# A two-layer recurrence on one core: a new order of work in the step, and input products in tiles of 64 stationary columns

## The chip, the core and the metric

The kernel runs on one core of a Trainium2 chip. The metric is device time of one launch in microseconds, the median of several runs. In this text PE is TensorE (matmuls), PEld its weight loads, DVE is VectorE, ACT is ScalarE, POOL is GpSimd and SP is SyncE, which here only issues DMAs. A "record" is one line of the trace for a matmul or a weight load: each fp32 matmul instruction of the program leaves two matmul records and two weight-load records.

## The reference, cut to what matters

Four layers follow each other, each added to its input (batch 32, 256 time steps, 256 features). The first two are recurrences over time and are what the change touches:

```python
# layer 0, for each t
z = sigmoid(x_t @ W_z + h @ U_z + vz)
r = sigmoid(x_t @ W_r + h @ U_r + vr)
hh = tanh(x_t @ W + (r * h) @ U + vh)
h = (1.0 - z) * h + z * hh            # x1_t = x_t + h
# layer 1, for each t
gate = sigmoid(g @ Wh.T + x1_t @ Wz.T + b)
g = tanh(g * (1 - alpha) + gate * x1_t)   # x2_t = x1_t + g
```

Layers 2 and 3 (a scan with forget and input gates, and an adapter with low-rank factors) have no loop over time on PE. They run after the recurrence and the change leaves them as they are.

## The kernel before

All arithmetic is fp32. The 256 features lie on 128 partitions in 2 halves (index m for an output half, k for an input half). A step t of layer 0 and a step t - 3 of layer 1 are done together (LAG is 3). The program unrolls 16 steps (BODY) in a hardware loop on DVE, ACT and POOL, and 4 steps (LOOP) in a hardware loop on PE.

**Tiles on PE.** For the recurrent products (`quarter`, L770) the stationary operand is a block of 128 rows by 32 columns of a weight, placed in one of four column positions, and the moving operand is the state, 128 by 32. One `quarter` is 4 matmuls, one for each position (8 records), and covers one (k, m). A step has 8 quarters of layer 0's gates r and z, 4 of the candidate and 4 of layer 1's gate: 16 quarters, 128 records. The products of the inputs (`ahead`, L714) don't depend on the state. They are made for two steps at once, so their moving operand is 128 by 64, with the same 32-column stationary blocks; per step they are 64 records (48 of `ahead_first` with wx, 16 of `ahead_second` with wz). They accumulate in PSUM on top of seeds (constants and biases) which ACT writes with copies (L333, L336, L339).

**Order on PE in a step** (`turn`, L824): the gates (`first_gates`, L778: half 0 of the state first, then half 1; then the rest, z last), one short piece of input products, layer 1's gate (`second_gate`, L797), the candidate (`first_cand`, L809) with 8 records of input products in the hole between its first and second quarter, and then the other input products, which stand between the candidate and the gates of the next step.

**The other engines.** ACT makes r from PSUM in two halves (L360), z (L362) and 1 - z by a second sigmoid with scale -1 (L363), layer 1's gate (L375), the candidate by tanh in two halves (L369), seeds, and layer 1's state by tanh (L380). DVE makes r h in two halves (L570), (1 - z) h (L572), gate times x1 (L602), the new state by two scans (L582), layer 1's sum by one scan (L608) and x1 (L596). POOL adds x2 (L267). Who waits for whom is written out by hand with semaphores; each engine runs its list in order. SP loads x for the input products in blocks of two steps, each released by the z products of an earlier step (L204), and x for the residual in blocks of eight steps (L196).

Of the kernel before, what the change touches and what calls it, by code (L numbers as in the profile page):

```python
# [13 lines left out]
HALVES, SLABS, BLK = 2, 4, 32  # L14
SLAB = D // SLABS
# [13 lines left out]
def build_program(nc, io):  # L29
# [3 lines left out]
    with ctx:  # L33
# [6 lines left out]
        def sem(name):  # L40
# [21 lines left out]
        keep_f = sb("keep_f", [P, HALVES, B])  # L62
# [29 lines left out]
        idle = sb("idle", [P, 2 * LAG])  # L92
# [25 lines left out]

        banks = [pb(f"bank{n}", [P, 512]) for n in range(8)]
# [11 lines left out]
        scanned, bits_set, seeds_ready, bias_done, hid_copied = (  # L131
            sem("scanned"), sem("bits_set"), sem("seeds_ready"), sem("bias_done"), sem("hid_copied"))
        seeded = sem("seeded")
# [19 lines left out]
        pad_done = sem("pad_done")  # L153
# [31 lines left out]
        def _(sp):  # L185
# [16 lines left out]
            def next_turn(n, others=()):  # L202
# [8 lines left out]
                next_steps(n, 1)  # L211


            next_turn(0, [(dst[:], io[name], tail_in) for dst, name in TAIL_LOADS])
# [42 lines left out]
        def _(pool):  # L257
            pool.memset(rin_g[:], 0.0).then_inc(pad_done, 1)

            pool.sem_inc(x2_done, 1)  # L260
            pool.sem_inc(y_done, FREE)

            def turn(n):
                for u in range(BODY):
                    s = n * BODY + u
                    pool.wait_ge(gate_pre, s + LAG + 2)
# [3 lines left out]
            with nc.Fori(0, TURNS, engines=bass.OrderedEngineSet([pool.engine]), hint_back_edge=True) as n:  # L270
                turn(n)
            pool.wait_ge(w2_used, 4)
# [43 lines left out]
        def _(act):  # L316
# [12 lines left out]
            def seed_reset(par, cands=None):  # L329
                for m in range(HALVES):  # L330
                    if cands is not None:
                        act.wait_ge(cand_done, cands + m)
                    act.activation(flat(pre_rh[par][m]), flat(seed_rh[:, m]), ACT.Copy).then_inc(seeded, 1)  # L333
# [4 lines left out]
            def seed_gate(par):  # L338
                act.activation(flat(pre_g[par]), flat(seed_g[:]), ACT.Copy).then_inc(seeded, 1)  # L339
# [3 lines left out]
            seed_reset(0)  # L343
            seed_keep(0)
            seed_reset(1)
            seed_gate(1)
# [9 lines left out]
            def gates_first(n, u):  # L356
                t, par, v = n * BODY + u, (u // STEPS) % 2, u % STEPS
                for m in range(HALVES):
                    act.wait_ge(r_pre, 2 * t + m + 1)
                    act.activation(r_f[:, m], pre_rh[par][m][:, 0, v, :], ACT.Sigmoid).then_inc(r_done, 1)  # L360
                act.wait_ge(z_pre, t + 1)
# [712 lines left out]
```

## Time and profile before

| | |
|---|---|
| median of 3 runs | 992.34 us (991.52 to 993.38) |
| profiled execution, its own time | 988.54 us |
| its span in the profile | 986.7 us |
| PEld busy | 763.6 us (77%) |
| ACT busy | 647.4 us (66%) |
| POOL busy | 203.3 us (21%) |

The profile's page gives for each engine the busy time, its share of the span and the number of instructions. The recurrence fills the first 612 us of the span; layers 2 and 3 fill the rest.

### The profile page before, as it was taken

What the parts mean: (1) busy time and instruction counts of PE and PEld (TensorE: products, weight loads), DVE (VectorE), ACT (ScalarE), POOL (GpSimd) and SP (SyncE); (2) the same over time, 40 slices, a digit from 0 to 9 for tenths busy, and PEclk for the clock granted to TensorE, in tenths of its full rate; (3) what the DMA queues carried; (4) which work ended last, traced back from release to release, by engine and by line L of the source; (5) the groups of instructions that cost most, each with busy time, mean ns of one, the idle gap of its engine ahead of it and who ended that gap; (6) DMA issues with size and microseconds to landing.
All of it is one profiled execution on the core that took longest, in us unless ns stands there. A gap on an engine that the chain in (4) does not pass through costs nothing.

```text
span 986.7 us, 112657 instructions
## 1 busy us (share of the span) xinstructions
PE 939.5 (95%) x50966; PEld 763.6 (77%) x50966; DVE 803.9 (81%) x2468; ACT 647.4 (66%) x2862; POOL 203.3 (21%) x390
## 2 busy tenths in 40 slices
PE   5699999999999999999999999959999999999986
PEld 5699999999999999999999998325555555555554
DVE  2378778878788778777878887799999999999993
ACT  2477777777777777777777776336455556555552
POOL 0011111111111111111111111223333223323330
PEclk7699999999999999999999999979999999999999
DMA  6113312310010100100101001100010000001001
GB/s 219 41 57 111 111 47 98 110 35 27 24 37 24 37 24 27 35 27 24 37 24 37 24 27 33 28 1 25 24 42 29 24 24 24 24 24 48 24 24 43
DMA packets 38295, 42.02 MB, mean 43 GB/s; under 512 B 5120, under 2 KB 31232, under 8 KB 37120
## 3 DMA queue, kind: packets, MB, share of 16 engines
q1 hardware_dynamic: 36832, 40.55, 13.3%
q10 hardware_dynamic: 1440, 1.18, 0.4%
q8 instruction: 12, 0.20, 0.1%
q14 instruction: 11, 0.09, 0.0%
HBM read 32.80 MB, written 8.91 MB: 42 GB/s over the span
## 4 chain that ended last, share of the span: by engine, by line
PE 55%; DVE 31%; issue 8%; ACT 4%; DMA 1%; ACTq 1%; DVEq 1%; POOL 0%; POOLq 0%
PE bank L772 30%; PE bank L718 22%; DVE arena L645 10%; DVE wx L657 4%; DVE cx L661 4%; ACT cand_kept L369 2%; DVE cx L670 2%; DVE cx L674 2%; DVE wx L643 2%; DVE cx L666 2%; DVE none_h L582 2%; DMA bias<-in_bias 1%; PE bank L890 1%; PE bank L907 1%; PE bank L861 1%
## 5 line engine op out<-in xcount | busy, mean ns | idle before, releaser
L718 PE MATMUL bank<-x_ahead,wx 128*32 128x64 f32 x12376 | 345.6, 224 | 6.4 <-ACT bank L336 3.2
L718 PEld LDWEIGHTS bank<-x_ahead,wx 128*32 128x32 f32 x12376 | 240.1, 111 | 3.3 <-issue 3.3
L772 PE MATMUL bank<-none_h,urz 128*32 128x32 f32 x16384 | 203.2, 199 | 8.6 <-issue 5.0
L772 PEld LDWEIGHTS bank<-none_h,urz 128*32 128x32 f32 x16384 | 180.8, 110 | 27.7 <-DVE none_h L582 13.2
L267 POOL TENSOR_TENSOR x<-x_f,h_gx 128x64 f32 x256 | 87.4, 341 | 529.9 <-PE bank L772 528.8
L890 PE MATMUL bank<-x,wl 128*128 (+1 forms) x384 | 180.9, 610 | 0.9 <-DVE rank_rows L624 0.9
L772 PE MATMUL bank<-rh_f,uh 128*32 128x32 f32 x8192 | 151.6, 199 | 5.0 <-DVE rh_f L570 2.2
L890 PEld LDWEIGHTS bank<-x,wl 128*128 128x128 f32 x384 | 68.7, 190 | 88.1 <-issue 88.1
L772 PEld LDWEIGHTS bank<-rh_f,uh 128*32 128x32 f32 x8192 | 122.7, 112 | 7.1 <-DVE rh_f L570 5.3
L582 DVE TENSOR_TENSOR_SCAN none_h<-zero_z,cand_kept 128x64 f32<-128x64 f32 x512 | 121.4, 278 | 5.4 <-ACT cand_kept L369 4.0
L380 ACT ACTIVATE h_gx<-h_pre 128x64 f32<-128x64 f32 x256 | 68.8, 269 | 80.8 <-DVE h_pre L608 80.8
L772 PE MATMUL bank<-h_gx,wh 128*32 128x32 f32 x8288 | 121.0, 198 | 0.7 <-ACT h_gx L380 0.7
L423 ACT ACTIVATE arena<-bank,bl 128x512 f32<-128x512 f32 x96 | 65.9, 687 | 77.5 <-PE bank L890 77.3
L570 DVE TENSOR_TENSOR rh_f<-r_f,none_h 128x32 f32<-128x32 f32 x512 | 82.4, 192 | 40.3 <-ACT r_f L360 19.3
L369 ACT ACTIVATE cand_kept<-bank 128x32 f32<-128x32 f32 x512 | 99.1, 202 | 21.0 <-PE bank L772 9.0
L645 DVE RECIPROCAL arena<-wx 128x512 f32<-128x512 f32 x32 | 107.3, 3353 | 1.1
L572 DVE TENSOR_TENSOR cand_kept<-keep_f,none_h 128x64 f32<-128x64 f32 x256 | 60.3, 235 | 58.6 <-ACT keep_f L363 56.9
L608 DVE TENSOR_TENSOR_SCAN h_pre<-zero_leak,h_gx 128x128 f32<-128x128 f32 x256 | 102.0, 399 | 0.1
L772 PEld LDWEIGHTS bank<-h_gx,wh 128*32 128x32 f32 x8288 | 95.6, 112 | 4.1 <-ACT h_gx L380 1.8
L718 PE MATMUL bank<-x_f,wz 128*32 128x64 f32 x4128 | 88.4, 223 | 0.0
L360 ACT ACTIVATE r_f<-bank 128x32 f32<-128x32 f32 x512 | 79.1, 190 | 9.4 <-PE bank L772 9.4
L279 POOL TENSOR_TENSOR arena<-arena 128x512 f32<-128x512 f32 x32 | 40.6, 1269 | 210.1 <-ACT arena L423 195.5
(87 smaller groups left out, 1290.0 us busy)
## 6 DMA issues: line engine op xcount, KB each, us to landing
x_in<-in_x SPq DMA_DIRECT2D x34, 256.0 KB, 2.7
x_ahead<-in_x SPq DMA_DIRECT2D x130, 64.0 KB, 1.9
arena<-in_w SPq DMA_DIRECT2D x8, 1024.0 KB, 5.7
out<-y SPq DMA_DIRECT2D x32, 256.0 KB, 2.5
rank_rows<-in_bias_rows SPq DMA_DIRECT2D x1, 1024.0 KB, 5.0
arena<-scratch SPq DMA_DIRECT2D x64, 16.0 KB
cx<-in_cx SPq DMA_DIRECT2D x1, 768.0 KB, 4.5
wx<-in_wx SPq DMA_DIRECT2D x1, 768.0 KB, 6.6
```

What stands on the lines that cost most here:

```text
L267: pool.tensor_tensor(x2[:, :, :, s], x1_f[:, u % LOOP], h1_gx[:, u % 2, :, :, 0], ALU.add).then_inc(x2_done, 1)
L360: act.activation(r_f[:, m], pre_rh[par][m][:, 0, v, :], ACT.Sigmoid).then_inc(r_done, 1)
L369: act.activation(cand_kept[:, u % 2, m, :, 0], pre_rh[par][m][:, 1, v, :], ACT.Tanh).then_inc(cand_done, 1)
L380: act.activation(h1_gx[:, at, :, :, 0], h1_pre[:, at, :, :, 1], ACT.Tanh).then_inc(h1_done, 1)
L423: act.activation(dst[:, unit], banks[(at + 2 * par) % 4][:], fun, bias=bl2[:, mat, unit:unit + 1]).then_inc(done, 1)
L570: dve.tensor_tensor(rh_f[:, m], r_f[:, m], none_h[:, now, m, :, 1], ALU.mult).then_inc(rh_done, 1)
L582: dve.tensor_tensor_scan(pairs(none_h, m), pairs(zero_z, m), pairs(cand_kept, m), 0.0, ALU.mult, ALU.add).then_inc(h_done, 1)
L608: dve.tensor_tensor_scan(flat(h1_pre[:, at]), flat(zero_leak[:]), flat(h1_gx[:, 1 - at]), 0.0, ALU.mult, ALU.add).then_inc(pre1_done, 1)
L645: dve.reciprocal(rec[:, k], s_t).then_inc(rec_done, 1)
L718: mm = pe.matmul(out[32 * j:32 * j + 32], weights(k, j, m), moving(k), start=False, stop=False, tile_position=(0, 32 * j), skip_group_chec ...
L772: mm = pe.matmul(out[32 * j:32 * j + 32], weights(k, j, m), moving(k), start=False, stop=k == 1, tile_position=(0, 32 * j), skip_group_che ...
L890: mm = pe.matmul(banks[(at + 2 * par) % 4][:], wl2[:, k, mat, unit], x2[:, k, bass.ds(p * GB, GB), :].rearrange("p q t -> p (q t)"), start ...
```

## The change

* **Tiles.** The input products go in stationary blocks of 64 columns instead of 32 (`WIDE`), two column positions instead of four, with half as many matmuls. Only the first block of the prologue keeps 32 columns. The weights wx and wz are copied once by POOL into the layout for that (`widen`, 8 copies, into the space of cx and of y), and PE waits for the 8 copies before its first step. The recurrent products keep blocks of 32 columns.
* **Order on PE.** Gates, then a block of input products (8 matmuls, 16 records), then the candidate, then layer 1's gate, then a second block of input products (16 records). No input product stands inside the gates or the candidate any more. In the gates both r quarters of state half 0 come first and the second r quarter of half 1 follows the first at once.
* **(z - 1) h.** The sigmoid of -z on ACT (L363) goes. DVE makes (z - 1) h from z by one instruction; the candidate's tanh has scale -1, and the state's scan subtracts.
* **Layer 1** moves half a step later on DVE and ACT: gate times x1 and its scan are done at the head of the next step on DVE, the tanh after r on ACT, and the matmuls for its gate behind the candidate's. x1 is made behind r h of the next step, without a wait of its own for layer 1's scan.
* **Seeds and waits.** The seeds of r and candidate go behind layer 1's gate on ACT, and PE waits for them (`reset_seeded`). POOL's x2 waits for z in place of layer 1's products. SP issues the second half's residual load of the turn before behind the fourth x block. r_done and cand_done are counted down by PE.

```diff
+WIDE = 2 * BLK
...
+        wx_wide = cx[:].rearrange("p k j g e -> p (k j g e)").rearrange("p (g k m n) -> p g k m n", g=3, k=HALVES, m=HALVES)
+        wz_wide = y[:, 0].rearrange("p h t -> p (h t)").rearrange("p (k m n) -> p k m n", k=HALVES, m=HALVES)
...
+                    if c == 3 and not first:
+                        next_steps(n - 1, 1)
...
+            def widen(dst, src):
+                slabs = lambda w: w.rearrange("p j (m c) -> p m j c", m=HALVES)
+                pool.tensor_copy(dst.rearrange("p m (j c) -> p m j c", j=SLABS), slabs(src)).then_inc(widened, 1)
+
+            pool.wait_ge(wx_in, 16)
+            pool.wait_ge(const_pre, 1)
+            for gate in (0, 2):
+                for k in range(HALVES):
+                    widen(wx_wide[:, gate, k], wx[:, k, :, gate])
+            pool.wait_ge(weights_in, 16 * len(WEIGHT_LOADS + SECOND_LOADS))
+            for k in range(HALVES):
+                widen(wz_wide[:, k], wz1[:, k])
+            for k in range(HALVES):
+                widen(wx_wide[:, 1, k], wx[:, k, :, 1])
...
+                    if last and u >= BODY - LAG - 1:
+                        pool.wait_ge(gate_pre, s + LAG + 2)
+                    else:
+                        pool.wait_ge(z_done, s + LAG + 2)
...
                 act.activation(zero_z[:, u % 2, :, :, 1], pre_z[par][:, :, v, :], ACT.Sigmoid).then_inc(z_done, 1)
-                act.activation(keep_f[:], pre_z[par][:, :, v, :], ACT.Sigmoid, scale=-1.0).then_inc(z_done, 1)
...
-                                   ACT.Tanh).then_inc(cand_done, 1)
+                                   ACT.Tanh, scale=-1.0).then_inc(cand_done, 1)
...
+                    t = n * BODY + u
+                    reset_gate(n, u)
+                    if not first or u > LAG:
+                        second_state(n, u)
+                    elif u:
+                        act.activation(idle[:, u:u + 1], var_eps[:], ACT.Copy).then_inc(h1_done, 1)
+                    update_gate(n, u)
+                    if u % STEPS == 0 and (u or not first):
+                        if first and u <= LAG + 1:
+                            act.wait_ge(gate_pre, u - 1)
+                        else:
+                            act.wait_ge(gate_done, t - LAG - 1)
+                        seed_gate(((u - STEPS) // STEPS) % 2)
+                    candidate(n, u)
+                    if not first or u >= LAG:
                         second_gate(n, u)
-                    candidate(n, u)
-                    t = n * BODY + u
                     if u % STEPS:
-                        seed_reset((u // STEPS) % 2, 2 * t + 2)
+                        if first and u < LAG:
+                            act.activation(idle[:, 0:1], var_eps[:], ACT.Copy).then_inc(idle_done, 1)
+                            act.wait_ge(idle_done, 1)
+                        else:
+                            act.wait_ge(gate_done, t - LAG + 1)
+                        seed_reset((u // STEPS) % 2, reset_seeded)
                     else:
-                        if second or u:
-                            act.wait_ge(z_done, 2 * t)
+                        if u or not first:
+                            act.wait_ge(z_done, t)
                         seed_keep(1 - (u // STEPS) % 2)
-                        if second:
-                            act.wait_ge(gate_done, t - LAG + 1)
-                        else:
-                            act.wait_ge(gate_pre, u + 1)
-                        seed_gate(((u - LAG) // STEPS) % 2)
-                    if second:
-                        second_state(n, u)
-                    else:
-                        act.activation(idle[:, u:u + 1], var_eps[:], ACT.Copy).then_inc(h1_done, 1)
...
+            def kept_state(n, u):
                 t, now = n * BODY + u, (u + 1) % 2
-                for m in range(HALVES):
-                    dve.wait_ge(r_done, 2 * t + m + 1)
-                    dve.tensor_tensor(rh_f[:, m], r_f[:, m], none_h[:, now, m, :, 1], ALU.mult).then_inc(rh_done, 1)
-                dve.wait_ge(z_done, 2 * t + 2)
-                dve.tensor_tensor(cand_kept[:, u % 2, :, :, 1], keep_f[:], none_h[:, now, :, :, 1],
-                                  ALU.mult).then_inc(kept_done, 2)
+                dve.wait_ge(z_done, t + 1)
+                dve.scalar_tensor_tensor(cand_kept[:, u % 2, :, :, 1], zero_z[:, u % 2, :, :, 1], 1.0,
+                                         none_h[:, now, :, :, 1], ALU.subtract, ALU.mult).then_inc(kept_done, 1)
...
-                                           0.0, ALU.mult, ALU.add).then_inc(h_done, 1)
-
-            def first_output(n, u, first):
+                                           0.0, ALU.mult, ALU.subtract).then_inc(h_done, 1)
...
-                    reset_state(n, u)
-                    if second:
+                    if not first or u > LAG:
                         second_gated(n, u)
+                        second_sum(n, u)
+                    reset_state(u)
+                    if u:
+                        first_output(n, u - 1, first)
+                    elif not first:
+                        first_output(n - 1, BODY - 1)
+                    kept_state(n, u)
                     next_state(n, u)
-                    if second:
-                        second_sum(n, u)
-                    first_output(n, u, first)
...
+            def ahead(out, weights, moving, width):
+
+                for k in range(HALVES):
+                    for at in range(0, P, width):
+                        mm = pe.matmul(out[at:at + width], weights(k, at), moving(k), start=False, stop=False,
+                                       tile_position=(0, at), skip_group_check=True)
                 return mm
...
+                narrow = lambda k, at: wx[:, k, at // BLK, gate, m * BLK:(m + 1) * BLK]
+                wide = lambda k, at: wx_wide[:, gate, k, m, at:at + WIDE]
+                return ahead(out.rearrange("p v b -> p (v b)"), narrow if first else wide,
+                             lambda k: x_ahead[:, par, :, k, :], BLK if first else WIDE)
...
+                    ahead(pre_g[par][:, m].rearrange("p v b -> p (v b)"), lambda k, at: wz_wide[:, k, m, at:at + WIDE],
+                          lambda k: x1_f[:, at:at + STEPS, k, :], WIDE)
...
+            pe.wait_ge(widened, 8)
...
                 pe.wait_ge(h_done, 1)
                 reset(0, 0)
-                keep(0, 0)
-                keep(0, 1)
+                pe.wait_ge(cand_done, 2)
+                reset(0, 1)
+                update(0, 0)
                 pe.wait_ge(h_done, 2)
-                reset(1, 0, taken=h_done).then_inc(r_pre, 1)
-                reset(0, 1)
+                reset(1, 0, taken=(h_done, cand_done)).then_inc(r_pre, 1)
                 reset(1, 1).then_inc(r_pre, 1)
-                keep(1, 0)
-                mm = keep(1, 1)
-                if late_keep:
-                    mm = late_keep()
-                mm.then_inc(z_pre, 1)
+                update(0, 1)
+                update(1, 0)
+                update(1, 1).then_inc(z_pre, 1)
...
                 pe.wait_ge(rh_done, 1)
                 cand(0, 0)
-                hole()
                 pe.wait_ge(rh_done, 2)
-                cand(1, 0).then_inc(cand_pre, 1)
-                cand(0, 1).then_inc(rh_done, -2)
+                cand(1, 0, taken=(rh_done, r_done)).then_inc(cand_pre, 1)
+                cand(0, 1)
                 cand(1, 1).then_inc(cand_pre, 1)
...
             def turn():
-                first_gates(0, late_keep=lambda: ahead_first(0, 1, 1, (1,)))
-                second_gate(0)
-                first_cand(0, hole=lambda: loaded(1, 0, 0, (0,)))
-                ahead_second(LOOP - STEPS, 1)
-                ahead_first(1, 0, 0, (1,))
-                ahead_first(1, 0, 1)
-
-                first_gates(1)
-                ahead_first(1, 2, 0, (0,))
-                second_gate(1)
-                first_cand(1, hole=lambda: ahead_first(1, 2, 0, (1,)))
-                ahead_first(1, 2, 1)
-                ahead_first(1, 1, 0)
-                ahead_first(1, 1, 1, (0,))
-
-                first_gates(2, late_keep=lambda: ahead_first(1, 1, 1, (1,)))
-                second_gate(2)
-                first_cand(2, hole=lambda: loaded(0, 0, 0, (0,)))
-                ahead_second(0, 0)
-                ahead_first(0, 0, 0, (1,))
-                ahead_first(0, 0, 1)
-
-                first_gates(3)
-                ahead_first(0, 2, 0, (0,))
-                second_gate(3)
-                first_cand(3, hole=lambda: ahead_first(0, 2, 0, (1,)))
-                ahead_first(0, 2, 1)
-                ahead_first(0, 1, 0)
-                ahead_first(0, 1, 1, (0,))
+                for u in range(LOOP):
+                    later = 1 - u // STEPS
+                    first_gates(u)
+                    if u % STEPS == 0:
+                        pe.wait_ge(ahead_loaded[later], 16)
+                        pe.wait_ge(reset_seeded, 2)
+                        ahead_first(later, 0, 0)
+                        ahead_first(later, 0, 1).then_inc(reset_seeded, -2)
+                    else:
+                        ahead_second((u - LAG) % LOOP, later)
+                    first_cand(u)
+                    second_gate(u)
+                    if u % STEPS == 0:
+                        ahead_first(later, 2, 0)
+                        ahead_first(later, 2, 1)
+                    else:
+                        ahead_first(later, 1, 0)
+                        ahead_first(later, 1, 1).then_inc(ahead_loaded[later], -16)
```

## Rows read from the trace of the kernel before

**Rows 1.** The page: busy time of two engines, share, instructions.
```profile
PE 939.5 (95%) x50966; PEld 763.6 (77%) x50966; DVE 803.9 (81%) x2468; ACT 647.4 (66%) x2862; POOL 203.3 (21%) x390
```

**Rows 2.** Windows: stretch; PE, PEld, DVE, ACT, POOL busy (instructions); granted clock; DMA.
```profile
42.00:586.00 544.00, 537.95 (x46254) 519.85 (x46258) 432.41 (x1925) 428.27 (x2411) 82.25 (x241) 1.00 0.15 45
```

**Rows 3.** Chain that ended last, 100 to 600 us, by line.
```profile
by line: PE bank L772 51.2%; PE bank L718 37.0%; ACT cand_kept L369 4.4%; DVE none_h L582 3.0%; issue 1.8%; DVE h_pre L608 0.9%; ACT r_f L360 0.6%; DVE rh_f L570 0.6%; ACTq L409 0.4%; ACT h_gx L380 0.1%
```

**Rows 4.** Timeline of PE, one step: start, length, engine, line, tiles, records.
```profile
303.12 0.74 PE L772 MATMUL bank<-none_h,urz 128*32 128x32 f32 x62
...
304.14 0.27 PE L772 MATMUL bank<-rh_f,uh 128*32 128x32 f32 x8
...
304.34 0.37 PE L772 MATMUL bank<-rh_f,uh 128*32 128x32 f32 x23
...
304.54 0.78 PE L718 MATMUL bank<-x_ahead,wx 128*32 128x64 f32 x39
305.37 0.77 PE L772 MATMUL bank<-none_h,urz 128*32 128x32 f32 x63
...
306.40 0.27 PE L772 MATMUL bank<-rh_f,uh 128*32 128x32 f32 x8
```

**Rows 5.** Timeline of DVE and of ACT beside it.
```profile
304.89 0.48 DVE L582 TENSOR_TENSOR_SCAN none_h<-zero_z,cand_kept 128x64 f32<-128x64 f32 x2
305.29 0.40 DVE L608 TENSOR_TENSOR_SCAN h_pre<-zero_leak,h_gx 128x128 f32<-128x128 f32 x1
...
306.15 0.35 DVE L570 TENSOR_TENSOR rh_f<-r_f,none_h 128x32 f32<-128x32 f32 x2
...
304.66 0.39 ACT L369 ACTIVATE cand_kept<-bank 128x32 f32<-128x32 f32 x2
...
305.93 0.36 ACT L360 ACTIVATE r_f<-bank 128x32 f32<-128x32 f32 x2
```

**Rows 6.** Groups with mean length: count, busy us, mean ns, idle before.
```profile
L718 PE MATMUL bank<-x_ahead,wx 128*32 128x64 f32 x12376 | 345.6, 224 | 6.4 <-ACT bank L336 3.2 <-issue 3.2
L772 PE MATMUL bank<-none_h,urz 128*32 128x32 f32 x16384 | 203.2, 199 | 8.6 <-issue 5.0
L582 DVE TENSOR_TENSOR_SCAN none_h<-zero_z,cand_kept 128x64 f32<-128x64 f32 x512 | 121.4, 278 | 5.4 <-ACT cand_kept L369 4.0
...
L907 PE MATMUL bank<-arena,wdown 128*128 128x256 f32 x256 | 58.1, 380 | 0.0
```

**Rows 7.** Timeline of PE after the recurrence, tiles of several sizes.
```profile
700.00 3.62 PE L907 MATMUL bank<-arena,wdown 128*128 128x256 f32 x16
703.54 1.13 PE L914 MATMUL bank<-wh,arena 64*128 64x256 f32 x8
704.61 3.70 PE L890 MATMUL bank<-x,wl 128*128 x8
708.24 0.64 PE L900 MATMUL bank<-arena,rin_g 128*32 128x256 f32 x8
708.81 1.98 PE L890 MATMUL bank<-x,wl 128*128 x4
```

**Rows 8.** The same stretch, weight loads.
```profile
704.61 0.30 PEld L890 LDWEIGHTS bank<-x,wl 128*128 128x128 f32 x2 [0.33 <-issue]
705.14 0.19 PEld L890 LDWEIGHTS bank<-x,wl 128*128 128x128 f32 x1 [0.24 <-issue]
705.57 0.19 PEld L890 LDWEIGHTS bank<-x,wl 128*128 128x128 f32 x1 [0.24 <-issue]
```

**Rows 9.** Prologue: timeline, DMA issues with time to landing, POOL's group.
```profile
4.42 0.47 ACTq L323 DMA_DIRECT2D wz<-in_wz  x1
...
17.16 0.96 PEld L772 LDWEIGHTS bank<-none_h,urz 128*32 128x32 f32 x64 [0.46 <-issue]
...
wz<-in_wz ACTq DMA_DIRECT2D x1, 256.0 KB, 9.3
...
L279 POOL TENSOR_TENSOR arena<-arena 128x512 f32<-128x512 f32 x32 | 40.6, 1269 | 210.1 <-ACT arena L423 195.5
```

More of the change, by code:

```diff
@@ L200, in next_steps, with next_turn @@
                              ).then_inc(x_loaded[s], 16)
-            def next_turn(n, others=()):
+            def next_turn(n, others=(), first=False):
                 for c in range(2, BLOCKS + 2):
@@ L210, in next_turn @@
                         sp.dma_start(dst, src).then_inc(done, 16)
-                next_steps(n, 1)
-            next_turn(0, [(dst[:], io[name], tail_in) for dst, name in TAIL_LOADS])
+            next_turn(0, [(dst[:], io[name], tail_in) for dst, name in TAIL_LOADS], first=True)
             for w in range(4):
@@ L327, in _, with seed_reset @@
             flat = lambda w: w.rearrange("p a v b -> p (a v b)")
-            def seed_reset(par, cands=None):
+            def seed_reset(par, done):
                 for m in range(HALVES):
-                    if cands is not None:
-                        act.wait_ge(cand_done, cands + m)
-                    act.activation(flat(pre_rh[par][m]), flat(seed_rh[:, m]), ACT.Copy).then_inc(seeded, 1)
+                    act.activation(flat(pre_rh[par][m]), flat(seed_rh[:, m]), ACT.Copy).then_inc(done, 1)
             def seed_keep(par):
@@ L410, in _ @@
                 turn(n)
-            for u in range(LAG):
-                second_gate(TURNS, u)
-                act.wait_ge(x2_done, T - LAG + u)
+            act.wait_ge(gate_done, T - LAG - 1)
+            seed_gate(1)
+            for u in range(LAG + 1):
+                act.wait_ge(x2_done, T - LAG - 1 + u)
                 second_state(TURNS, u)
+                if u < LAG:
+                    second_gate(TURNS, u)
             def evict(p, par, unit, mat, first=False):
@@ L712, in recur, with ahead_first @@
                 return mm
[L714 to L719 removed]
+            def ahead(out, weights, moving, width):
[3 more added lines that the diff above has]
+                                       tile_position=(0, at), skip_group_check=True)
                 return mm
[L722 removed]
+            def ahead_first(par, gate, m, first=False):
                 out = (pre_rh[par][m][:, 0], pre_z[par][:, m], pre_rh[par][m][:, 1])[gate]
[L725 to L727 removed]
+                narrow = lambda k, at: wx[:, k, at // BLK, gate, m * BLK:(m + 1) * BLK]
+                wide = lambda k, at: wx_wide[:, gate, k, m, at:at + WIDE]
+                return ahead(out.rearrange("p v b -> p (v b)"), narrow if first else wide,
+                             lambda k: x_ahead[:, par, :, k, :], BLK if first else WIDE)
             def ahead_second(at, par):
                 for m in range(HALVES):
[L732 to L733 removed]
+                    ahead(pre_g[par][:, m].rearrange("p v b -> p (v b)"), lambda k, at: wz_wide[:, k, m, at:at + WIDE],
+                          lambda k: x1_f[:, at:at + STEPS, k, :], WIDE)
             col = lambda w: (lambda k, j, m: w[:, k, j, m * BLK:(m + 1) * BLK])
@@ L756, in _ @@
             pe.wait_ge(seeded, 3)
-            for gate, m in ((0, 0), (0, 1), (2, 0), (2, 1)):
-                ahead_first(0, gate, m)
-            ahead_first(0, 1, 0)
-            ahead_first(0, 1, 1, (0,)).then_inc(ahead_loaded[0], -16)
+            for gate, m in ((0, 0), (0, 1), (1, 0), (1, 1), (2, 0), (2, 1)):
+                mm = ahead_first(0, gate, m, first=True)
+            mm.then_inc(ahead_loaded[0], -16)
             pe.wait_ge(hidden_in, 16 * len(HIDDEN_LOADS))
@@ L768, in _, with quarter @@
             pe.wait_ge(weights_in, 16 * len(WEIGHT_LOADS + SECOND_LOADS))
-            def quarter(out, weights, moving, k, m, taken=None):
+            pe.wait_ge(widened, 8)
+            def quarter(out, weights, moving, k, m, taken=()):
                 for j in range(SLABS):
@@ L868, in _ @@
             pe.wait_ge(x1_done, T + 1)
+            pe.wait_ge(gate_seeded, T // STEPS)
             ahead_second(LOOP - STEPS, 1)
-            pe.wait_ge(z_done, 2 * T)
+            pe.wait_ge(z_done, T)
             pe.wait_ge(hid_done, 2)
```

98 lines of the change are left out of this document (42 added, 56 removed).

## The prediction

> **What bounds the kernel now.** The page's first part has PE busy for 95% of the span and DVE for 81% [rows 1]. A mean over stages says little, so the windows come next: over 544 us of the recurrence PE is busy 537.95 us at a granted clock of 1.00, that is 2.4 GHz. POOL runs one instruction in a step there, 241 in that window, so a step takes 544 / 241 = 2.257 us [rows 2]. The chain of waits puts 88% of the recurrence on matmuls, 51% on recurrent and 37% on input products, and some 9% on tanh, scan and sigmoid [rows 3]. The reader is to see a kernel in which PE's queue is nearly always the last to be ready, with layer 0's own chain close behind.
>
> Matmuls are pipelined, so what a record costs is its distance to the next. Recurrent records: 23 in 0.37 us, less the last one's 0.20 us, are 7.7 to 7.9 ns each; 62 of the gates in 0.74 us, with waits inside, are 8.9 ns. Input records: 39 in 0.78 us, less 0.22 us, are 14.7 ns [rows 4, 6]. Four column positions share these, so one position gives an input product (64 moving columns) every 59 ns. With 128 * 8.4 + 64 * 14.7 ns = 2.02 us a step, 0.24 us are left over: waits for the state, first loads behind a wait, and the end of PE's loop, where PE stands for 0.27 us (last input record at 304.54 + 0.78 - 0.22 = 305.10, next gates at 305.37) though the first scan was over at 304.89 + 0.28 = 305.17 [rows 4 to 6].
>
> **Layer 0's chain after the change.** From the first gate record to the first candidate record it is 306.40 - 305.37 = 1.03 us (32 gate records, sigmoid at 305.93, r h at 306.15) [rows 4, 5]. As many records stand ahead of the first r as before, so I leave it. From the candidate on: one quarter of 8 records 0.07, from the second quarter to the tanh 304.66 - 304.34 = 0.32, to the scan 0.23, the first scan 0.28, and 0.05 handed over (an estimate, out of the same 0.23): 0.95 us. The hole of input products (304.14 to 304.34 for the first quarter, now 0.07) is gone, 0.13 us less. The chain could so run in 1.98 us a step [rows 4 to 6]. If it set the end, the change would win. The question is what PE needs.
>
> **Tiles of 64 columns.** Input products halve in number, 64 records to 32. The moving operand stays at 64 columns and a position gives a result every 59 ns. A record's cadence doesn't depend on the width of its tile: on full 128-column tiles 16 records with 256 moving columns take 3.62 - 0.38 us over 15 steps, 216 ns, which is 54 ns for 64 columns [rows 6, 7]. Two positions in place of four with half the records: 8 rounds of 59 ns are 0.47 us for a block of 16, as 32 narrow ones take (32 * 14.7 = 0.47). I cost the halving at 0 gained. Bounds: 54 ns a round would give 0.04 us a block back; two wide tiles that don't run beside each other would add 0.47 us a block. The two 64-row tiles do run in pairs (8 records of 216 ns in 1.13 us) [rows 7], so I take pairs.
>
> **The switch between tile sizes.** Today the recurrence has one tile size. Afterwards each step goes 32, 64, 32, 64: four switches. Behind the recurrence the trace shows switches. The 16 records of L907 start at 700.00, the last at 703.24; the next form starts at 703.54, 0.30 later where the cadence is 0.216. The end of one form is 0.06 to 0.08 us behind the start of the next at all four borders: 703.62 against 703.54, 704.67 against 704.61, 708.31 against 708.24, 708.88 against 708.81 [rows 7]. Inside the recurrence a form starts 0.16 us or more before the last one's end: the candidate at 304.14 runs to 304.41 and the next candidate form starts at 304.34, with input products between [rows 4]. So at a switch PE lets the array drain until 0.07 us before the record's end. And the first load isn't hidden: behind the border at 704.61 the second load comes 0.53 us later, then 0.43 apart, 0.10 us for 128 columns [rows 8]; for 32 columns, two rounds of 216 ns in 0.64 - 0.40 us leave 0.02 [rows 7]. For 64 I take 0.05, in between.
>
> The Trainium skill ("TensorEngine Tiling (Array Packing)", Key Properties) says that a change of the tiling mode, not of the tile alone, drains TensorE, and lists 128x64 and 128x32 as separate configurations. By it the four switches cost what the rows above show for other pairs; without it the sum is that of the first rival. No row here shows the pair 32 and 64.
>
> **PE's sum.** Narrow stretch (gates, or candidate and layer 1's gate, 64 records): first load 0.02, 63 * 8.4 ns = 0.53, then 0.20 - 0.07 = 0.13 to the switch: 0.68. Wide stretch: first load 0.05, 7 rounds 0.41 and 0.01, then 0.22 - 0.07 = 0.15: 0.62. Twice both: 2.60 us a step. At PE's loop end the 0.27 us of today replace a 0.15, once in four steps: 0.03. So 2.63 us, against the chain's 1.98: from gates to candidate PE needs 1.30 where the chain is ready at 1.03. All the time that the shorter chain gives is lost to PE, and it is late by 0.37 us a step: 256 * (2.63 - 2.257) = 95 us. Ends: 7.7 ns a record and free first loads, 2.47 us, 55 us more; 8.9 ns and first loads of 0.10, 2.75 us, 126 us more. I take the middle of the cadences, as the gates' 8.9 has waits in it that are then satisfied early.
>
> **The other edits.** The second sigmoid on ACT goes and DVE's instruction for (z - 1) h takes its place with nothing added; both lie beside PE, 0 today and after. If PE weren't last, DVE would be near: scan half 1 starts at 305.09, gate times x1 then needs 0.29 and the sum 0.40, so r h could start at some 306.0, where it starts at 306.15 [rows 5]; with 2.63 us a step 0.3 us more are free. Layer 1's loop (gate, product, sum, tanh) has a step's time and fits both. PE's new wait for the seeds has queued behind it the wide block and the candidate; ACT writes them after layer 1's gate, 0.8 us before PE asks, so 0. SP's x loads go out on the same signal two steps ahead; the moved residual load waits for an x1 of the turn before, long done. POOL's x2 has no follower on the path. Prologue: the last weights land at 4.42 + 9.3 = 13.7 us; four copies are left to POOL then, 128x256 each, between nothing and the 1.27 us of a 128x512 operation; at 0.7 they end at 16.5, before the gates' 17.16 [rows 9]. Cost 0; at 1.27 each they end at 18.8, 1.6 us late. Layer 1 ends half a step later: 1 us. Layers 2 and 3 unchanged.
>
> **Sum.** The profiled execution took 988.54 us, 1.8 more than its span of 986.7, and the median is 3.8 above it. 988.5 + 95 + 1 = 1084.5, so 1088 on the median's scale; the ends are 1049 and 1121.
>
> **Rivals.** (1) *The chain is freed and the switch is free* (32 and 64 columns count as one mode). PE then needs 128 * 8.4 + 32 * 29.4 ns = 2.02 us, the chain 1.98; meeting twice a step, with PE's loop end, 2.10 us: 40 us less, 953. It decides as soon as a switch costs under 0.03 us. For it: no row shows this pair. Against it: all four borders in rows 7 drain, whichever side changes, rows or columns.
> The Trainium skill ("TensorE: Matmul & The Clock Gate", Back-to-back issue gap) gives small matmuls a floor of some 25 ns from start to start. By that, 32 records fewer would give 0.8 us a step back; the trace disagrees, with 7.9 ns between recurrent records.
> (2) *The switch is cheap but not free* (half of what rows 7 show, as the drain of a short record may be shorter): 2.3 us, 11 us more, 1004. For it: rows 7 have only records of 256 and 512 moving columns. Against: the 0.07 us is the same for both.
> (3) *Wide tiles don't pair*: 0.47 us more in each of two blocks, 3.57 us a step, 1330. Against it the pairs of 64 rows [rows 7].
>
> **How the numbers follow.** Forecast 0.67, first rival 0.22, second 0.06, third 0.05. Predicted 1088, own range 1049 to 1121. To leave out no more than 2 in 10 the range must reach the first rival, so it goes from 950 to 1118. Faster by over 0.2% (what a measurement of this kernel can tell from no change) 0.22, within 0.2% 0.01, slower 0.77.
>
> **What would show it.** Right: in the changed profile a wide block begins some 0.13 us after the last narrow record's start and a narrow one 0.15 us after the last wide one's; 16 wide records span 0.47 us; the gates' weight loads never wait for DVE; the chain is over 95% PE; a step is near 2.6 us. Wrong: narrow records run on within 0.01 to 0.03 us behind wide ones, the chain has DVE and ACT in a third of it, and a step is near 2.1 us. Single wide records every 59 ns would be the third rival. A prologue whose first gates start after 19 us would show the copies.

## The result, and the profile after

The changed kernel takes 1108.47 us (median of 4 runs, 1107.11 to 1110.29) against 992.86 before on the same chip: a ratio of 1.117, 95% interval 1.1146 to 1.1195. That is slower, as forecast, and 20 us beyond the 1088 that I named, inside the range. Its profiled execution took 1110.29 us with a span of 1108.5, 121.8 us more than the span before.

The page's first part answers to [rows 1]. The span and the instruction count stand above it:

```profile
span 1108.5 us, 95068 instructions
...
PE 1070.9 (97%) x42766; PEld 857.6 (77%) x42766; DVE 782.9 (71%) x2465; ACT 591.5 (53%) x2606; POOL 204.2 (18%) x398
```

PE has 8,200 matmul records fewer and is busy 131 us longer. The windows answer to [rows 2] (PE, PEld, DVE, ACT, POOL busy, granted clock):

```profile
42.00:700.00 658.00, 658.00 (x38342) 605.94 (x38334) 411.30 (x1916) 372.72 (x2156) 79.75 (x240) 1.00 0.12 37
```

POOL still counts the steps: 240 in 658 us, 2.74 us each, where it was 2.257. PE is busy in all of the window at a granted clock of 1.00, so its clock, the upper level of 2.4 GHz, is no part of the loss. The chain of waits over the recurrence (100 to 600 us, and the same shares from 100 to 700) answers to [rows 3]:

```profile
by line: PE bank L809 55.2%; PE bank L754 44.8%
```

Nothing but matmuls is left in it. Who waits is told by the waits of the same stretch (who, for whom: us in total, times, longest), which have no row for PE any more; the first line here is the kernel before's, the others are the changed kernel's:

```profile
PEld bank L772 <- DVE none_h L582: 11.6, 55, 0.3
```
```profile
POOL x L290 <- ACT zero_z L386: 439.4, 182, 2.5
DVE none_h L617 <- ACT cand_kept L392: 116.8, 182, 0.6
ACT cand_kept L392 <- PE bank L809: 106.0, 182, 0.7
ACT r_f L381 <- PE bank L809: 86.7, 182, 0.6
DVE rh_f L602 <- ACT r_f L381: 56.1, 171, 0.3
```

One step of PE, answering to [rows 4] (start, length, engine, line, tiles, records; the view ends inside the last form, so its 50 are not all of its 64):

```profile
401.81 0.81 PE L809 MATMUL bank<-none_h,urz 128*32 128x32 f32 x64
402.56 0.69 PE L754 MATMUL bank<-x_ahead,cx 128*64 128x64 f32 x16
403.17 0.46 PE L809 MATMUL bank<-rh_f,uh 128*32 128x32 f32 x32
403.44 0.57 PE L809 MATMUL bank<-h_gx,wh 128*32 128x32 f32 x32
403.94 0.69 PE L754 MATMUL bank<-x_ahead,cx 128*64 128x64 f32 x16
404.56 0.63 PE L809 MATMUL bank<-none_h,urz 128*32 128x32 f32 x50
```

The reader is to see the four borders. The last gate record starts at 401.81 + 0.81 - 0.20 = 402.42 and the wide block at 402.56, 0.14 us later (these times are rounded; record by record the trace has 0.126 us). The last wide record starts at 402.56 + 0.69 - 0.23 = 403.02 and the candidate at 403.17, 0.15 us later (0.152). As with the borders of [rows 7], a form starts 0.06 to 0.08 us before the end of the one ahead: 402.62 against 402.56, 403.25 against 403.17, 404.01 against 403.94, 404.63 against 404.56. Where the size stays, the next record comes at once: candidate and layer 1's gate, both 32 columns, overlap by 0.19 us (403.63 against 403.44).

DVE and ACT beside it answer to [rows 5]:

```profile
403.86 0.47 DVE L617 TENSOR_TENSOR_SCAN none_h<-zero_z,cand_kept 128x64 f32<-128x64 f32 x2 [0.65 <-ACT cand_kept L392]
...
402.40 0.29 ACT L381 ACTIVATE r_f<-bank 128x32 f32<-128x32 f32 x2 [0.31 <-PE bank L809]
...
403.62 0.36 ACT L392 ACTIVATE cand_kept<-bank 128x32 f32<-128x32 f32 x2 [0.50 <-PE bank L809]
```

The first half of the state is there at 403.86 + 0.28 = 404.14, the gates start at 404.56. The shorter chain is real, and PE comes 0.4 us behind it.

### The profile page after: what moved, and what is told of

Read it like the earlier page. It is cut to its first block, busy times and chain, and to the rows that moved or that the text cites. A ratio compares the mean times of both kernels' runs of the same rounds, so it can differ in the third digit from the quotient of the medians.

```text
span 1108.5 us, 95068 instructions
## 1 busy us (share of the span) xinstructions
PE 1070.9 (97%) x42766; PEld 857.6 (77%) x42766; DVE 782.9 (71%) x2465; ACT 591.5 (53%) x2606; POOL 204.2 (18%) x398
## 4 chain that ended last, share of the span: by engine, by line
PE 66%; DVE 25%; issue 5%; DMA 1%; ACT 1%; DVEq 1%; ACTq 1%
PE bank L809 35%; PE bank L754 28%; DVE arena L681 9%; DVE wx L693 4%; DVE cx L697 4%; DVE cx L706 2%; DVE cx L710 2%; DVE wx L679 2%; DVE cx L702 2%; DMA bias<-in_bias 1%; PE bank L910 1%; PE bank L927 1%; PE bank L880 1%; DVE arena L714 0%; ACT L381 0%
## 5 line engine op out<-in xcount | busy, mean ns | idle before, releaser
L754 PE MATMUL bank<-x_ahead,cx 128*64 128x64 f32 x6144 | 265.3, 229 | 1.0 <-issue 1.0
L754 PEld LDWEIGHTS bank<-x_ahead,cx 128*64 128x64 f32 x6144 | 212.0, 138 | 16.9 <-issue 1.1
L290 POOL TENSOR_TENSOR x<-x_f,h_gx 128x64 f32 (+1 forms) x256 | 85.5, 334 | 638.7 <-ACT zero_z L386 630.9
L809 PE MATMUL bank<-h_gx,wh 128*32 128x32 f32 x8288 | 146.8, 203 | 0.8 <-ACT h_gx L403 0.8
L809 PEld LDWEIGHTS bank<-h_gx,wh 128*32 128x32 f32 x8288 | 125.5, 109 | 2.2 <-ACT h_gx L403 1.6
L809 PE MATMUL bank<-rh_f,uh 128*32 128x32 f32 x8192 | 118.2, 199 | 3.4 <-issue 2.0
L809 PEld LDWEIGHTS bank<-rh_f,uh 128*32 128x32 f32 x8192 | 89.5, 112 | 21.0 <-issue 2.1
L754 PE MATMUL bank<-x_f,y 128*64 128x64 f32 x2064 | 88.5, 228 | 0.0
L754 PEld LDWEIGHTS bank<-x_f,y 128*64 128x64 f32 x2064 | 70.7, 137 | 5.3
L398 ACT ACTIVATE gate_f<-bank 128x64 f32<-128x64 f32 x256 | 57.4, 224 | 32.1 <-PE bank L809 2.9
```

The source lines that it names most:

```text
L290: pool.tensor_tensor(x2[:, :, :, s], x1_f[:, u % LOOP], h1_gx[:, u % 2, :, :, 0], ALU.add).then_inc(x2_done, 1)
L398: act.activation(gate_f[:], pre_g[(s // STEPS) % 2][:, :, s % STEPS, :], ACT.Sigmoid).then_inc(gate_done, 1)
L754: mm = pe.matmul(out[at:at + width], weights(k, at), moving(k), start=False, stop=False, tile_position=(0, at), skip_group_check=True)
L809: mm = pe.matmul(out[32 * j:32 * j + 32], weights(k, j, m), moving(k), start=False, stop=k == 1, tile_position=(0, 32 * j), skip_group_che ...
```

## The experiments

Ratios are to the kernel before, run beside each kernel on one chip; its medians there were 991.2 to 991.7 us, so times of different groups can be compared to within a few microseconds. The first four vary the number of switches between tile sizes.

**The new order with narrow tiles.** No switch; all else as changed.
```diff
-                return ahead(..., narrow if first else wide, ..., BLK if first else WIDE)
+                return ahead(..., narrow, ..., BLK)
...
-            pe.wait_ge(widened, 8)
```


> The changed kernel with its new order, its (z - 1) h and its waits, but every input product in tiles of 32 columns again (no POOL copies). Theory S (the switches between tile sizes are the loss): no switch is left, so 4 * 0.14 to 0.15 us go from each step of 2.75 us; the step is 2.10 to 2.20 us, the time 955 to 985, below the kernel before. Rival O (the new order is the loss, PE waits more or its narrow records run slower in it): still over 1060.


Measured: 998.60 us, 1.0067 (1.0046 to 1.0088). The tiles are the loss: 110 of its 116 us. But the order brought no gain either. My bounds of 955 to 985 were missed, by 14 us or more: steps of 2.19, 2.28, 2.19 and 2.50 us (the starts of the state's scans), not 2.10.

**Two wide blocks put together in even steps.**
```diff
                         ahead_first(later, 0, 1).then_inc(reset_seeded, -2)
+                        ahead_first(later, 2, 0)
+                        ahead_first(later, 2, 1)
...
-                        ahead_first(later, 2, 0)
-                        ahead_first(later, 2, 1)
```


> The changed kernel with the two wide blocks of each even step put together ahead of the candidate: three switches a step on average instead of four, the same matmuls. Theory S: a pair of switches costs 0.126 + 0.152 - 0.008 - 0.028 us and about 0.05 of first loads, 0.29 us, every second step: 0.14 us a step, 37 us less than the change, 1072. Rival O: the order is nearly the same, so 1108 within 5 us, or slower where the longer block delays the candidate.


Measured: 1124.39 us, 1.1335 (1.1314 to 1.1356), slower than the change by 16 us. The 1072 of theory S was missed, and not even its sign came true; of rival O only the clause "slower where the longer block delays the candidate" did. PE's timeline of that kernel, from an even step into the odd one, and the even step after it:

```profile
400.22 0.57 PE L809 MATMUL bank<-h_gx,wh 128*32 128x32 f32 x32
400.99 0.70 PE L809 MATMUL bank<-none_h,urz 128*32 128x32 f32 x58 [0.20 <-DVE none_h L617]
...
403.74 0.82 PE L809 MATMUL bank<-none_h,urz 128*32 128x32 f32 x64
404.48 1.15 PE L754 MATMUL bank<-x_ahead,cx 128*64 128x64 f32 x32
405.56 0.46 PE L809 MATMUL bank<-rh_f,uh 128*32 128x32 f32 x32
```

A pair of switches went, but nothing stands between layer 1's gate and the next gates any more. PE waits there for the scan: last record at 400.22 + 0.57 - 0.20 = 400.59, next at 400.99. And the candidate of an even step starts 405.56 - 403.74 = 1.82 us after the gates, where it was 403.17 - 401.81 = 1.36 in the changed kernel and the chain would allow 1.03 [rows 4]. The sum comes out: a wait of 0.39 us less a pair of switches (0.28 as expected) is 0.11 us in two steps, and two steps take 2.40 + 3.21 = 5.61 us here against 5.49, some 15 us over 128 pairs. So the drains do cost what they were priced at. The block had covered the chain; moving it to save a switch uncovered it.

**Only the first block wide.** Two switches a step.
```diff
-                return ahead(..., narrow if first else wide, ..., BLK if first else WIDE)
+                return ahead(..., narrow if first or gate else wide, ..., BLK if first or gate else WIDE)
```


> The changed kernel with its order kept, the first block of input products wide and the second (candidate and z) in tiles of 32 columns: two switches a step instead of four, twice the records in the second block. Theory S: 0.276 us a step less, 1108 - 70 = 1038. A rival that the number of instructions sets the time (PE's issue): 16 records more a step, slower than 1108. Rival O: 1108 within 5 us.


Measured: 1059.32 us, 1.0674 (1.0651 to 1.0698). Direction and cause of theory S hold, 49 us instead of 70. More instructions a step and yet faster, so the number of instructions isn't what costs here. Three of four steps lose 0.27 to 0.30 us (2.45 to 2.47 against 2.747), as expected; the fourth takes 2.73. There, where PE's loop ends, the gates start 0.27 us after the last input record; this gap is in the kernel before too and not in the changed one (more below).

**The old order with wide tiles.** Six switches.
```diff
-                ahead_first(0, gate, m)
+                ahead_first(0, gate, m, first=True)
...
+                wide = lambda k, at: wx_wide[:, gate, k, m, at:at + WIDE]
+                return ahead(..., narrow if first else wide, ..., BLK if first else WIDE, parts)
```


> The kernel before with its old order, and only the tiles of the input products made wide (with POOL's copies): six switches a step, as its input products stand in three places. Theory S: 6 * 0.14 us on a step of 2.26, less 0.1 us of waits that are filled: 3.0 us, 992 + 190 = 1180. Rival O (the order is the loss): near 992. A rival that wide tiles gain by themselves: under 990.


Measured: 1156.17 us, 1.1655 (1.1633 to 1.1677), 24 us under the 1180 expected. With 0, 2, 4 and 6 switches a step stand 998.6 (991.7 in the old order), 1059.3, 1108.5 and 1156.2 us. Each pair adds 48 to 61 us, 0.19 to 0.24 us a step; in the old order, three pairs add 164 us, 55 each. That is less than the 0.28 us priced for a pair. From 0 to 2 switches a drain takes the place of a wait for seeds (0.08 us in every second step), from 2 to 4 the gap at PE's loop end goes (0.27 in every fourth; both below); from 4 to 6 the order changes too.

**(z - 1) h alone, in the old order.**
```diff
-                act.activation(keep_f[:], ..., ACT.Sigmoid, scale=-1.0).then_inc(z_done, 1)
...
-                dve.tensor_tensor(cand_kept[...], keep_f[:], none_h[...], ALU.mult)
+                dve.scalar_tensor_tensor(cand_kept[...], zero_z[...], 1.0, none_h[...], ALU.subtract, ALU.mult)
```


> The kernel before with (z - 1) h from z alone as its only edit: no second sigmoid on ACT, one DVE instruction in place of another, the tanh with scale -1. Forecast: the sigmoid lies beside PE's work, so 0, 990 to 994. A rival that ACT's place was in the way of the candidate's tanh or of the seeds: up to 5 us faster.


Measured: 991.44 us, 1.0001 (0.9992 to 1.0011). Nothing, as forecast.

**Why the narrow records came late.** In the kernel with new order and narrow tiles PE is busy 99% of the recurrence, with the matmuls of the kernel before, and still a step takes 2.19 us at best where my cadences sum to 2.02. Layer 1's gate, 32 records, runs from first to last in 0.36 us right behind the candidate and took 0.27 in the kernel before, behind input products. Two kernels ask why. The first is the narrow one with a piece of input products between candidate and layer 1's gate:

```diff
+                    ahead_first(later, gate, 0, parts=(0,))
                     second_gate(u)
+                    ahead_first(later, gate, 0, parts=(1,))
```


> The new order with narrow tiles (998.6 us), and 8 records of the second block of input products put between the candidate and layer 1's gate. In the traces layer 1's gate takes 0.335 us from its first to its last records where it stands right behind the candidate, and 0.244 us behind a wait or an input product. Theory P (narrow records beyond the 32nd in a row without a pause or a slower piece run late): the piece cures it, 0.09 us a step on PE, part of it lost to the chain: 975 to 985. Rival C (layer 1's gate is slow for what runs on ACT and DVE at that time): 998 to 1002, with the same spacing in the block.


Measured: 997.46 us, 1.0059 (1.0041 to 1.0077). The 975 to 985 expected was missed: layer 1's gate needs 0.33 us, better by 0.03, not cured. Two steps of four are down to 2.14 us. The gain went at once into a wait of PE behind the gates of even steps, 0.19 us instead of 0.08.

The second is the changed kernel, with its four switches, and layer 1's gate ahead of the candidate:

```diff
-                    first_cand(u)
                     second_gate(u)
+                    first_cand(u)
```


> The changed kernel with layer 1's gate ahead of the candidate (the wide blocks and the four switches stay). Theory P: the slow place is a place in the run of narrow records, so the candidate now has the spacing of 42 to 85 ns per four records and layer 1's gate 32; the time stays at 1108 within 6 us. Rival C: layer 1's gate keeps its slow spacing, or both are fast and 0.09 us a step (23 us) are gained, 1085. The candidate comes 0.25 us later, where PE is late anyway.


Measured: 1101.97 us, 1.1118 (1.1095 to 1.1141), 6.5 us under the changed kernel (5 by the ratios), where theory P allowed 6 and rival C asked for 23. PE's timeline of this kernel:

```profile
402.69 0.46 PE L809 MATMUL bank<-h_gx,wh 128*32 128x32 f32 x32
402.97 0.51 PE L809 MATMUL bank<-rh_f,uh 128*32 128x32 f32 x32
```

Layer 1's gate now takes 0.46 us and the candidate 0.51, where they took 0.57 and 0.46. The slow place went over to whatever stands behind the first 32 narrow records. So theory P holds for the place. It isn't all: the second block is slower by 0.05 instead of 0.11 us here, and why the amounts differ is open.

**PE's loop.** The narrow kernel with the new order, 16 steps in PE's loop in place of 4.
```diff
-            with nc.Fori(0, T // LOOP, ...):
-                turn()
+            with nc.Fori(0, T // (4 * LOOP), ...):
+                for _ in range(4):
+                    turn()
```


> The new order with narrow tiles, and PE's hardware loop of 16 steps instead of 4, nothing else. In the trace of that kernel the steps take 2.19, 2.28, 2.19 and 2.50 us, the last one at PE's loop end. If the loop end is what makes the last one long, three of four become 2.19 to 2.28 and the time is 980 to 985; if the long step comes from something else (DVE's and ACT's own loop end, code loading), 995 to 1000 or slower.


Measured: 1851.46 us. The instruction queue's row on its page, above that of the kernel with the loop of 4:

```profile
q8 instruction: 405, 6.64, 1.4%
```
```profile
q8 instruction: 12, 0.20, 0.1%
```

From 100 to 600 us the chain of waits gives "issue", time in which PE waited for nothing that the profile shows, half of the time:

```profile
by line: issue 49.6%; PE bank L793 27.1%; PE bank L739 23.3%
```

405 loads are some 25 in each of 16 iterations: PE's instructions are loaded anew in each, and that PE stands for them is the reading that fits. My expectation had code loading as a cause of "slower", not of nearly twice the time. Whether the loop end makes the fourth step long isn't told by this run.

**z's products first.** The wait of PE behind the gates of even steps I took for the one for r's seeds: in the two narrow kernels ACT's copies of these end at 404.08 and 404.25, and PE goes on at 404.23 and 404.40, 0.15 us later in both. Here z's products stand ahead of the candidate (their seeds are written right after z in the odd step), r's behind it; the piece between stays.
```diff
+                    if u % STEPS:
+                        act.wait_ge(z_done, t + 1)
+                        seed_keep((u // STEPS) % 2)
...
-                        pe.wait_ge(reset_seeded, 2)
-                        ahead_first(later, 0, 0)
-                        ahead_first(later, 0, 1).then_inc(reset_seeded, -2)
+                        ahead_first(later, 1, 0)
+                        ahead_first(later, 1, 1)
```


> Narrow tiles and the new order with the piece between candidate and layer 1's gate, and two blocks of input products exchanged: z's go ahead of the candidate (their seeds are written right after z in the odd step), r's and the candidate's behind it. In the traces of the two narrow kernels PE stands 0.08 and 0.19 us after the gates of every even step, which I put down to ACT's late seeds for r. If that is so, some 0.1 us a step pair on average goes: steps of 2.14 to 2.18 beside the two long ones, 980 to 988, under the kernel before. If the seeds weren't it, 995 to 1000.


Measured: 987.28 us (8 runs), 0.9962 (0.9947 to 0.9977): under both kernels, by 0.4% under the one before. PE's timeline:

```profile
400.04 0.53 PE L739 MATMUL bank<-x_ahead,wx 128*32 128x64 f32 x23
400.68 0.71 PE L793 MATMUL bank<-none_h,urz 128*32 128x32 f32 x59
...
402.53 0.53 PE L739 MATMUL bank<-x_ahead,wx 128*32 128x64 f32 x22
402.83 0.80 PE L793 MATMUL bank<-none_h,urz 128*32 128x32 f32 x63
...
405.01 0.79 PE L793 MATMUL bank<-none_h,urz 128*32 128x32 f32 x63
```

The wait is gone, and the exchange of two blocks is what took it away: gates start at 402.83 and 405.01, and three steps of four take 2.17 us. The fourth takes 2.47. At PE's loop end the last input record starts at 400.04 + 0.53 - 0.22 = 400.35 and the gates at 400.68, 0.33 us in place of 0.01. It isn't the wait for the state: both halves of the scan were done at 399.99 + 0.47 = 400.46. The gap comes once in four steps, as PE's loop does (the other engines' loops have 16 steps); no run has a longer loop without the loading, so that the loop end is its cause is argued, not shown. Without the gap the kernel would stand at some 987 - 64 * 0.3 = 968 us (an estimate).

**A loop of 8.** The kernel with z's products first, 8 steps in PE's loop.
```diff
+            with nc.Fori(0, T // (2 * LOOP), ...):
+                for _ in range(2):
+                    turn()
```


> The kernel with z's products first, PE's hardware loop of 8 steps instead of 4. A loop of 16 steps had 405 instruction loads (6.6 MB) in place of 12 and 1851 us. If the loop of 8 still fits where PE keeps its instructions, one loop end in two goes, 0.3 us in 8 steps: 8 to 10 us less than the loop of 4. If it doesn't, far slower, 1200 or more.


Measured: 1908.90 us, 421 instruction loads (6.90 MB). That is some 13 loads in each of 32 iterations, half as many as with the loop of 16 and its twice as long body. A loop of 4 steps stays loaded, one of 8 doesn't; lengths between weren't run.

**Everything in tiles of 64 columns.** No switch, and 96 records a step where the change has 160.
```diff
-                for j in range(SLABS):
-                    mm = pe.matmul(out[32 * j:32 * j + 32], ..., tile_position=(0, 32 * j), ...)
+                for j in range(2):
+                    mm = pe.matmul(out[WIDE * j:WIDE * j + WIDE], ..., tile_position=(0, WIDE * j), ...)
```


> The changed kernel with every product of the recurrence in tiles of 64 columns, the recurrent ones too (weights laid out so in the inputs, no POOL copies): no switch between tile sizes, 64 + 32 records a step. If a position still gives a recurrent record every 29 ns, 64 * 14.6 + 32 * 28 ns = 1.83 us a step and the chain of 2.0 sets the end: 940 to 970. If the load of 64 columns sets the pace (the first wide load costs 0.05 us, so 53 to 58 ns a position), 64 * 28 + 32 * 28 ns = 2.69 us a step: 1085 to 1105. I take the second. Either way the four drains are gone.


Measured: 1125.12 us, 1.1361 (1.1329 to 1.1394), the second of the two cases and 20 us beyond its 1105: a step takes 2.80 us, not 2.69. PE's timeline:

```profile
402.36 0.69 PE L741 MATMUL bank<-x_ahead,wx 128*64 128x64 f32 x16
402.85 1.10 PE L793 MATMUL bank<-none_h,urz 128*64 128x32 f32 x32
403.76 0.69 PE L741 MATMUL bank<-x_ahead,wx 128*64 128x64 f32 x16
```

Two things are to be seen. Without a change of size there is no drain: 402.85 is 0.20 us before the end of the block ahead (403.05), where it would be 0.07 behind a change. And 32 recurrent records take 403.76 - 402.85 = 0.91 us, 28.4 ns each, close to the (402.85 - 402.36) / 16 = 30.6 ns of records with twice the moving columns. Two positions share them, so one position gives a result every 57 and every 61 ns. With half the moving columns and hardly a gain, something that belongs to the 64 stationary columns sets the pace; their load is the likely one, not shown by itself. The Trainium skill ("TensorE: Matmul & The Clock Gate", LDWEIGHTS) gives a load the time of its columns at 1.2 GHz, 53 ns for 64; by that rule the pace would be the load's, and the trace is 4 to 8 ns above it.

## Why the prediction was right, point by point

* **Tiles of 64 columns bring nothing on PE.** Right. 16 wide records span 0.69 - 0.23 = 0.46 us, 0.47 forecast. They pair, so the third rival is out.
* **The switch.** Right, and closely: 0.13 us out of a narrow stretch and 0.15 out of a wide one were forecast from borders of other sizes behind the recurrence; the changed kernel has 0.126 and 0.152, record by record. The Trainium skill ("TensorEngine Tiling (Array Packing)", Key Properties) has a change of tiling mode drain TensorE; the trace agrees for 32 and 64 columns too, 0.07 us before the record's end. The first rival (no price) and the second (half of it) are out by these borders, and by the three of four steps that lose 0.27 to 0.30 us with a pair of switches.
* **PE's sum: the narrow stretch was mis-sized.** Forecast 0.55 us from the first to the last of 64 records, first load included. The gates need 0.61 and candidate with layer 1's gate 403.44 + 0.57 - 0.20 - 403.17 = 0.64. Together 0.15 us a step, 38 us in all. The cadence of 8.4 ns was the middle between 7.9 ns (23 records of the candidate) and 8.9 (62 of the gates), taken because the gates' stretch was said to have waits in it. Without any such wait the gates now need 0.61 / 63 = 9.7 ns a record. I had found 0.24 us a step left over in the kernel before, called them waits and first loads, and then took them out of the sum for the kernel after. Part of them was this: records behind the first 32 in a row come late. Record by record, the gates' first 32 span 0.27 us, and from there to the last it is 0.35, of which the last four distances alone are 0.09; the candidate spans 0.26 and layer 1's gate behind it 0.37. Why is open.
* **PE's loop end.** Forecast 0.03 us a step; it is not there. The steps are alike: gates at 401.81 and 404.56, and the scans are 2.746 to 2.747 us apart in each of four places. In the kernel with a narrow second block it shows again. A wide block leaves PE's sequencer time to get ahead, is my reading, not shown by itself. The forecast had 8 us too many here, which by luck hid part of the term above.
* **The step.** 2.60 + 0.15 is the measured 2.75. Against the measured 2.246 (scan to scan) that is 128 us over 256 steps, where the span grew by 121.8; the first 32 steps grew by only 8.6 us instead of 16. There, from 20 to 110 us, the chain of waits gives "issue" 10.8% in the kernel before and 4.6% in the changed one; what PE stands for in it is not shown.
* **The range.** Its ends, 2.47 and 2.75 us a step, don't come out of the terms named for them: 7.7 ns a record and free first loads give 2 * (0.62 + 0.57) + 0.03 = 2.41 us, 8.9 ns and first loads of 0.10 give 2 * (0.79 + 0.67) + 0.03 = 2.95. The measured 2.75 is inside either way, but at the very end of the one that was stated.
* **The chain.** Its terms hold within 0.06 us: from the first gate record to the sigmoid 402.40 - 401.81 = 0.59 us (0.56 before [rows 4, 5]), from the candidate's first record to the tanh 403.62 - 403.17 = 0.45 (0.39 forecast), on to the scan 0.24 (0.23), and 0.4 us are then free. But no kernel here got near 1.98 us a step: the first rival's 953 us was priced with the same 8.4 ns. The kernel that has what it asked for, the order without switches, takes 998.6, and the shortest step seen with the loop of 4 is 2.14.
* **The other edits.** (z - 1) h is 0 (991.44). POOL's last two copies start at 14.46 and end at 15.2, before PE's first gates at 17.34, where it was 17.16 [rows 9], so they hide as forecast. The seeds' wait was 0 in the changed kernel as forecast, but 0.08 to 0.19 us in even steps once PE got faster, as the narrow kernels show.

## What to carry to other kernels

Count the changes of tile size in PE's order of work before counting matmuls: each one costs the last record's length less 0.07 us (0.13 us behind a record of 0.20, 0.15 behind one of 0.22), and a pair in each step added 0.2 us or more to a step of 2.2. Look for the price in the kernel's own trace, where another stage changes sizes; here it was right to 0.01 us. Look too at what the moved block had covered: putting two blocks together saved a switch and uncovered a longer wait. And what the sum of cadences leaves unexplained before the change belongs into the sum after it, until a row shows that it goes.

## What the runs showed of the hardware

* A change between tiles of 32 and 64 stationary columns lets the next record start 0.07 us before the end of the last one (0.126 us after its start behind a narrow record, 0.152 behind a wide one); without a change it starts 0.18 to 0.20 us before the end.
* PE's loop of 4 steps (768 matmul records) runs with 12 instruction loads in the whole execution; one of 8 steps has 421 and one of 16 has 405, and the kernel needs 1909 and 1851 us instead of 987 and 999. PE's mean granted clock fell to 0.80 and 0.84 with the stops.
* Where a run of narrow records starts behind a pause or a drain, the first 32 are 8 ns apart; in the next 8 the distance rises (to about 11 ns), whichever weights they use: the gates', layer 1's gate's or the candidate's.
* With 64 stationary columns in every tile a position gives a result every 57 ns for 32 moving columns and every 61 ns for 64, nearly alike.
* Where PE's loop ends, the gates start 0.27 to 0.33 us after the last record of narrow input products, in five kernels; behind a wide block there is no such gap. That the loop end causes it is not shown.
